# LoRA units of W0 made in pairs, with the products by A's low half on 64 rows of TensorE each

## The reference

```
delta = lora_B @ lora_A * 0.5                 # 1024x64 times 64x1024
w     = quantize(weight + delta)              # to a codebook, with scales per group of 128
x = x + x @ (w + delta).T                     # layer 0
x = x + x @ W1.T + 2 * gated LoRA experts     # layer 1
x = x + x @ W2.T + b + 2 * adapter LoRA       # layer 2
x = x + x @ W3[adapter].T                     # layer 3
```

## Time and profile before

| | |
|---|---|
| median of 3 runs | 674.18 us (673.72 to 674.28) |
| the profiled execution's own time | 673.76 us |
| its span | 671.9 us |
| TensorE busy (matmuls) | 665.5 us, 99%, 3296 instructions |
| TensorE weight loads | 571.0 us, 85% |
| VectorE, ScalarE, GpSimd busy | 351.6, 278.3, 91.9 us |
| TensorE's granted clock | 0.999 of full speed over the span |

### The profile page before, as it was taken

One profiled execution on the slowest core, in us unless ns is written; L12 is line 12 of the kernel. 1 busy time (PEld: TensorE's weight loads), 2 busy tenths in 40 slices (PEclk: granted clock), 3 DMA queues, 4 the chain that ended last, 5 costly groups with the idle time before them and its releaser, 6 DMA issues.

```text
span 671.9 us, 9271 instructions
## 1 busy us (share of the span) xinstructions
PE 665.5 (99%) x3296; PEld 571.0 (85%) x3296; DVE 351.6 (52%) x535; ACT 278.3 (41%) x414; POOL 91.9 (14%) x120
## 2 busy tenths in 40 slices
PE   8999999999999999999999999999999999999998
PEld 7899989999999988888888888889888888888886
DVE  5799899879961384114544223661421653411453
ACT  5565574962812371214552122553121564121353
POOL 3210225005010030001120000230000221000120
PEclk9999999999999999999999999999999999999999
DMA  9662112001000503002874001777000586000372
GB/s 320 174 202 63 47 31 63 1 1 63 1 1 0 188 19 132 0 1 96 296 228 155 0 0 34 263 237 239 0 0 0 190 284 216 23 0 1 101 233 105
DMA packets 39202, 67.33 MB, mean 100 GB/s; under 512 B 3524, under 2 KB 22980, under 8 KB 39172
## 3 DMA queue, kind: packets, MB, share of 16 engines
q1 hardware_dynamic: 34576, 58.68, 26.7%
q10 hardware_dynamic: 4596, 8.26, 3.7%
HBM read 58.54 MB, written 8.39 MB: 100 GB/s over the span
## 4 chain that ended last, share of the span: by engine, by line
PE 98%; DVE 1%; DMA 1%; ACT 0%; issue 0%
PE ps L1010 30%; PE ps L1011 30%; PE ps L1012 30%; PE ps L1111 3%; PE ps L1113 1%; PE ps L1144 1%; DMA w_w<-w 1%; PE ps L1023 1%; PE ps L1025 0%; DVE e_both L737 0%; PE ps L1160 0%; PE ps L1152 0%; DVE ring_lo L737 0%; DVE tmp L999 0%; ACT e_mid_w L564 0%
## 5 line engine op out<-in xcount | busy, mean ns | idle before, releaser
L1010 PE MATMUL ps<-e_both,ring_hi 128*128 128x384 f32 (+3 forms) x384 | 133.7, 348 | 1.2 <-DVE e_both L737 1.2
L737 DVE TENSOR_TENSOR ring_lo<-raw,ring_hi 128x512 fp32r<-128x512 f32 x128 | 90.9, 725 | 82.7 <-ACT ring_hi L649 82.5
L1012 PE MATMUL ps<-e_both,ring_lo 128*128 128x384 f32 (+3 forms) x384 | 133.4, 347 | 0.0
L649 ACT ACTIVATE ring_hi<-raw 128x512 fp32r<-128x512 f32 x128 | 79.4, 629 | 70.2 <-PE ps L1012 66.6
L1010 PE MATMUL ps<-x_both,e_both 128*128 128x512 f32 x256 | 101.5, 397 | 0.0
L1011 PE MATMUL ps<-x_both,e_both 128*128 128x512 f32 x256 | 101.2, 395 | 0.0
L1010 PE MATMUL ps<-ring_hi,e_mid 128*128 128x512 f32 x256 | 101.0, 395 | 0.0
L1012 PE MATMUL ps<-ring_hi,e_mid 128*128 128x512 f32 x256 | 101.0, 395 | 0.0
L1011 PE MATMUL ps<-ring_lo,e_mid 128*128 128x512 f32 x256 | 101.0, 394 | 0.0
L1012 PE MATMUL ps<-x_both,e_both 128*128 128x512 f32 x256 | 101.0, 394 | 0.0
L498 POOL TENSOR_TENSOR raw<-raw,ident 128x128 f32<-128x128 f32 x64 | 43.3, 679 | 315.9 <-DMA raw<-w_t 315.9
(11 more groups left out here) (148 smaller groups left out, 864.1 us busy)
## 6 DMA issues: line engine op xcount, KB each, us to landing
raw<-w_t SPq DMA_DIRECT2D x64, 512.0 KB, 3.6
xraw<-x_t SPq DMA_DIRECT2D x16, 512.0 KB, 4.8
w_w<-w SPq DMA_DIRECT2D x15, 512.0 KB, 4.4
y<-tmp ACTq DMA_DIRECT2D x30, 256.0 KB, 2.5
e_both_w<-w_t SPq DMA_DIRECT2D x5, 512.0 KB, 8.7
e_mid_w<-bs SPq DMA_DIRECT2D x24, 64.0 KB, 2.8
e_both_w<-w_t SPq DMA_DIRECT2D x3, 384.0 KB, 6.0
w_w<-w SPq DMA_DIRECT2D x2, 256.0 KB, 5.2
```

The lines of the kernel that those rows point to most:

```text
L649: act.activation(ring_hi[:, (2 * k + h) % 4, :], raw[:, k % RAW, h * 512:(h + 1) * 512], ACT.Copy).then_inc(w3_hi, 1)
L737: return dve.tensor_tensor(out, whole, hi.bitcast(F32), ALU.subtract)
L1010: pe.matmul(out, a[0], b_[0], start=start, stop=False, **kw)
L1012: return pe.matmul(out, a[1], b_[0], start=False, stop=stop, **kw)
```

## The change

- A call `lora(u)` now makes units u and u + 1. It is called after chunk 2 for u = 0 and u = 2, and then after chunks 3, 5, 8, 11, 15 and 19 for u = 4, 6, 8, 10, 12 and 14.
- Within a call, each of the two k-tiles has four matmuls: the two over 128 rows (one for each unit), then the two by A's low part. Of these the first reads partitions 0 to 63 (`stack_b` and `stack_al`) and the second partitions 64 to 127 (`b_below` and `stack_al`), and they write different banks.
- `stack_al` holds A's low part in both halves, made by one VectorE instruction over 128 partitions where there were 64. `b_below` is a second copy of B's high part in partitions 64 to 127, one more ScalarE instruction ahead of the split of A. GpSimd's zeros and their semaphore are gone.
- Units 2 and 3 write banks 5 and 1. A call waits for all earlier units' copies when u is 4 or more. Chunk 3 (bank 5) waits for three copies, `br(2)` (bank 1) for four. The copies wait for TensorE as before; the count goes up by two at the end of a call.

```diff
-LORA_AFTER = {3: 4, 4: 5, 5: 6, 6: 7, 8: 8, 9: 9, 11: 10, 12: 11, 15: 12, 16: 13, 18: 14, 19: 15}
+LORA_AFTER = {3: 4, 5: 6, 8: 8, 11: 10, 15: 12, 19: 14}
+LORA_BANK = [6 + u % 2 if u not in (2, 3) else {2: 5, 3: 1}[u] for u in range(16)]
...
-        stack_b, stack_a, stack_al = bc_hi, bc_lo, x_pair[:, 1, :]
+        stack_b, stack_a, stack_al, b_below = bc_hi, bc_lo, x_pair[:, 1, :], x_pair[R0:P, 0, :]
...
-                elif item[0] == "lora":
-                    pool.wait_ge(lora_hi, 2)
-                    pool.memset(stack_al[R0:P, :].bitcast(F32), 0.0).then_inc(lora_clear, 1)
-                    pool.wait_ge(lora_clear, 1)
...
                     act.activation(stack_b[0:R0, :], xraw[0:R0, 0, :], ACT.Copy).then_inc(lora_hi, 1)
+                    act.activation(b_below, xraw[0:R0, 0, :], ACT.Copy).then_inc(lora_twice, 1)
...
-                    minus(stack_al[0:R0, :], xraw[0:R0, 1, :], stack_a[0:R0, :]).then_inc(lora_lo, 1)
+                    minus(stack_al, xraw[:, 1, :], stack_a[:, :]).then_inc(lora_lo, 1)
...
             def lora(u):
                 p, q = divmod(u, 4)
-                if u >= 2:
-                    pe.wait_ge(delta_out, u - 1)
+                if u >= 4:
+                    pe.wait_ge(delta_out, u)
                 a_cols = slice(2 * P * p, 2 * P * (p + 1))
                 for i in range(2):
-                    k = 2 * q + i
-                    out, b_cols = ps[:, 6 + u % 2, 2 * P * i:2 * P * (i + 1)], slice(k * P, (k + 1) * P)
-                    pe.matmul(out, stack_b[:, b_cols], stack_a[:, a_cols], start=i == 0, stop=False,
+                    out = [ps[:, LORA_BANK[u + v], 2 * P * i:2 * P * (i + 1)] for v in range(2)]
+                    b_cols = [slice(k * P, (k + 1) * P) for k in (2 * q + i, 2 * q + 2 + i)]
+                    for v in range(2):
+                        pe.matmul(out[v], stack_b[:, b_cols[v]], stack_a[:, a_cols], start=i == 0, stop=False,
+                                  skip_group_check=True)
+                    pe.matmul(out[0], stack_b[0:R0, b_cols[0]], stack_al[0:R0, a_cols], start=False, stop=True,
                               skip_group_check=True)
-                    ins = pe.matmul(out, stack_b[:, b_cols], stack_al[:, a_cols], start=False, stop=True,
+                    ins = pe.matmul(out[1], b_below[:, b_cols[1]], stack_al[R0:P, a_cols], start=False, stop=True,
                                     skip_group_check=True)
-                ins.then_inc(delta_mm, 1)
+                ins.then_inc(delta_mm, 2)
...
                 if c == 2:
                     pe.wait_ge(br_down, 1)
+                    pe.wait_ge(delta_out, 4)
...
+                if n == 3:
+                    pe.wait_ge(delta_out, 3)
...
                 if n == 2:
                     pe.wait_ge(lora_lo, 2)
-                    pe.wait_ge(lora_clear, 1)
-                    for u in range(4):
-                        lora(u)
+                    pe.wait_ge(lora_twice, 1)
+                    pe.wait_ge(br_down, 1)
+                    lora(0)
+                    lora(2)
```

More of the change, by code:

```diff
@@ L239, in build @@
         lora_lo = sem("lora_lo")
-        lora_clear = sem("lora_clear")
+        lora_twice = sem("lora_twice")
         delta_mm = sem("delta_mm")
@@ L529, in delta @@
                 act.activation(delta_of(p)[:, 2 * q:2 * q + 2, :],
-                               ps[:, 6 + u % 2, :].rearrange("p (k t) -> p k t", t=2 * P), ACT.Copy,
+                               ps[:, LORA_BANK[u], :].rearrange("p (k t) -> p k t", t=2 * P), ACT.Copy,
                                scale=0.5).then_inc(delta_out, 1)
```

## The result

The changed kernel takes 677.65 us (median of 6 runs, 677.46 to 677.79) against 673.84 us for the kernel before (6 runs): ratio 1.0056, 95% interval 1.0046 to 1.0067. It is slower by 3.8 us, where 2.2 us faster was forecast. The profiled spans are 675.8 and 671.9 us, so the profiles hold the whole difference.

What follows compares the result with a forecast made beforehand. One stream of matmuls on TensorE was taken to bound the kernel. Stall -0.38, products by A's low half -1.9, new waits +0.05 gave -2.2 us, so 671.8 us, range 671.3 to 677.3.

Steps and rivals of the forecast that it cites:

- What bounds the kernel: Whole kernel: one stream of matmuls on TensorE, busy 99% of the span, with three waits of 3.0 us in all.
- The stall: Before unit 2, waiting for bank 6 to be copied out: the wait goes with banks 5 and 1, -0.38 us.
- The products by A's low half: In the units, 16 couples of 64-row matmuls run side by side: -1.9 us, bounded by 0 and 1.9.
- rival 1: At the couples: no overlap, or only their loads limit them; switches free; 673.1 to 673.8 us; chance 0.28.
- Going between 128 rows and 64: In each group of four, 32 switches in all: taken as 0 us each, upper end 0.27 us each.
- the break-even of 0.07 us: At the changes of rows: the price of a switch above which the kernel is slower, 2.2 / 32.
- Rival 2: At each change of rows TensorE drains, loads kept ahead: 0.16 us each, +2.9 us, 677.1 us; chance 0.19.
- rival 3: At each change of rows the drain also exposes the loads: 0.27 us each, 680.6 us; chance 0.09.
- New waits: Pairs waiting for all earlier copies, tightest at pair 6/7 for unit 5's copy: 0 to 0.1 us lost, 0.05 put.
- Splits ahead of the units: Before the first unit: one more ScalarE copy of 1.04 us, covered by 2.1 us, so no cost.
- Does it last: From the units to the end of the kernel: the gain is kept, no loss counted.

Runs made afterwards that it cites:

- e1: The changed kernel with the products by A's low half over all 128 rows again, zeros below; 673.33 us, ratio 0.9994 to the kernel before.
- e9: The changed kernel without its 64-row form: all matmuls over 128 rows, A's low half in both halves, no second copy of B; 673.37 us.
- e4: The changed kernel with both matmuls of a couple on rows 0 to 63, so they cannot run side by side; 679.63 us.
- e6: As e1, but the products by A's low half have 32 stationary columns, with 32 changes of columns there and back; 673.14 us.
- e5: The changed kernel with 32 stationary columns instead of 128 in each 64-row matmul; 676.30 us.
- e8: The changed kernel with units 0 to 3 in one call, eight 128-row matmuls then four couples; other units over 128 rows; 673.47 us.
- e3: The changed kernel with 128-row and 64-row matmuls alternating within each group: 64 changes of rows, no couples; 687.86 us.

## Why the prediction was wrong

**What bounds the kernel**: right. The list of waits has a fourth entry that I passed over (0.2 us, for a DMA at the start); it changes nothing.

**The stall** (-0.38 us): right in kind, too small by 0.10. It was worth 0.48 us in the trace, since the load behind it was exposed too; that 0.10 is the same cost that decided the case at the changes of rows. Its wait is gone and no copy is late. e1 and e9 measure 0.4 us under before, with intervals that reach to no change.

**The products by A's low half** (-1.9 us, from 0 to 1.9): right at the end taken. Starts lie within 0.01 us and e4 gives 2.0 us. The two loads of a couple also start together, so the bound by loads in rival 1 does not apply. The Trainium skill gives, in "TensorE: Matmul & The Clock Gate", "Part 3: Packing small matmuls", starts some 4 ns apart for matmuls on different rows; the rows (0 to 0.01 us) agree.

**Going between 128 rows and 64** (0 us taken, 0 to 0.27 kept): this is the step that failed. The row that I called the nearest, 128*128 to 128*32, shows a change of columns, and such a change is free even 32 times over (e6). A change from 128 rows to 64 or back costs 0.19 us, 32 of them 6.2 us; with the stall at its measured size, -0.48 - 1.9 + 6.2 = +3.8. I had the place, the break-even of 0.07 us and both prices around the true one, and gave rivals 2 and 3 together 0.28. The forecast rested on likeness of form between two rows that differ in just the respect that mattered; "no row shows a change of rows" should have weighed against taking 0.

The size lies between the rivals since each had one half of it. Rival 2 took the wait for the modelled end of the matmul before, 0.16 us, and kept the loads ahead; rival 3 exposed the load too, 0.27. In fact the load is exposed (0.10 us, e5), and the wait before it is shorter than modelled: the load starts 0.20 to 0.22 us after the last matmul's start, not 0.28, so about 0.09 us beyond the distance. The Trainium skill says in "TensorEngine Tiling (Array Packing)", "Key Properties", that a change of the tiling mode drains TensorE; it gives no price. The change to 64 rows agrees with it. The changes to 32 columns and to 96 rows cost nothing, and no row shows whether they are changes of the mode at all. So I was wrong to read the free column change as evidence against the rule: it need not have been a case of it.

**New waits** (+0.05 us): right for this kernel, no wait came. Pair 6/7 and the copy of unit 5 in the changed kernel, against the earlier trace rows:

```profile
51.48 0.40 PE L1024 MATMUL ps<-bc_lo,bc_hi 128*128 128x256 f32 x2
...
49.48 0.60 ACT L527 ACTIVATE raw<-ps 128x512 f32<-128x512 f32 x1
```

The pair came 1.1 us later than unit 6 had, the copy ended 1.4 us ahead of it. The copy itself started 0.8 us later than before, so its start does hang on TensorE, against what I assumed. The stream was late here, which hid how tight the place is: in e9 the copy is 0.66 us ahead of the pair, and in e8 the wait is real, 0.28 us.

**Splits ahead of the units** (0): right. VectorE's low part of A ran over 128 partitions from 24.24 for 1.23 us, the same price as over 64, and ended 1.9 us before the first unit.

**Does it last:** what is lost or won in the units reaches the end: each experiment's total moved by what its groups moved, within 0.3 us, with e8's wait and e3's slow clock counted in.

## What to carry to other kernels

Running two 64-row matmuls side by side is real and saves a whole distance, but going into the 64-row form and out of it again costs 0.19 us each way here, since the stream stops and the next load is exposed. Count the changes and not the matmuls: with 256 columns a run of couples has to be four long before it repays them (4 x 0.12 against 0.39). So gather all 64-row work, or fill the idle rows with zeros and stay in one form. Gathering has a price of its own: results come out later, and in e8 the next wait for a copy took back more than the couples had saved. And when a price is taken from the nearest row, ask in which respect that row differs from what is added.

## What had not been expected of the hardware

- A stream can lose 4 us with no entry in the waits and the busy share unchanged at 99%: the distances between starts show it, and a duration of 0.38 in place of 0.28 marks the exposed load.
- In e3, where each of the sixteen matmuls of units 0 to 3 had a stop of 0.19 us behind it, the granted clock was then 0.50 from 32 to 38 us, 3.0 us more. With the stops at every second place (the changed kernel) the clock stayed at 1.00. One trace shows this; the link is argued.
- Matmuls over 96 of 128 rows, or with 32 of 128 columns, go in and out of the stream for nothing.
- A stall costs more than its wait: the load behind it is exposed too, 0.10 us (the stall before unit 2, and pair 6/7 in e8).
